# Side products of the attention stages: one clump at the end of each quad's period, in place of four points within it

## The reference, cut to what matters

```
L0: h = layernorm(x)*(1+scale)+shift; q = h Wq; c = h Wkd; k, v = c Wku, c Wvu; rope(q, k)
    y = softmax(mask(q k^T / sqrt(32))) v, 16 heads of 32, causal by blocks of 128; x += y Wo
L1: h = rms(x)*w*(1+scale); q, k, v = h Wq, h Wk, h Wv; rope; 8 heads of 64 on one k and v; x += y Wo
    x += (silu(h Wg) * (h Wu)) Wd
L2: h = layernorm(x)*..+..; q, k, v = h Wqkv; q, k normalised per head; 16 heads of 32
    x += gamma1 * (softmax(q k^T + bias) v Wproj + b);  x += gamma2 * MLP(layernorm(x)..)
L3: per expert: gelu(x W1 + b1) W2 + b2; silu(layernorm(..)) out_W; x += ..
```

## Time and profile before

| | us |
|---|---|
| median of 3 runs | 3025.26 (3024.14 to 3026.44) |
| the profiled execution | 3025.34 |
| its span | 3023.6 |

### The profile page before, as it was taken

One profiled execution on the slowest core, in us unless ns is written; L12 is line 12 of the kernel. 1 busy time (PEld: TensorE's weight loads), 2 busy tenths in 40 slices (PEclk: granted clock), 3 DMA queues, 4 the chain that ended last, 5 costly groups with the idle time before them and its releaser, 6 DMA issues.

```text
span 3023.6 us, 33071 instructions
## 1 busy us (share of the span) xinstructions
PE 2668.8 (88%) x13120; PEld 1592.8 (53%) x13120; DVE 1250.7 (41%) x2490; ACT 1152.7 (38%) x2423; POOL 241.4 (8%) x220
## 2 busy tenths in 40 slices
PE   6588988999999679999996799999997599998787
PEld 1144444544555268888883344444453288885333
DVE  1146545434434444344431346354554544442222
ACT  0256565544434321111112357465664422222332
POOL 2123213101210000000001000000000000001000
PEclk8879999999999889999998799989999799999989
DMA  8000000000000010000001000000000000000000
GB/s 292 14 1 1 1 1 22 1 8 8 8 1 1 21 42 21 22 21 22 22 1 75 1 1 1 1 1 1 1 1 29 14 29 29 15 1 28 14 14 28
DMA packets 33514, 61.27 MB, mean 20 GB/s; under 512 B 3136, under 2 KB 15984, under 8 KB 32848
## 3 DMA queue, kind: packets, MB, share of 16 engines
q1 hardware_dynamic: 29280, 45.63, 4.5%
q0 software_dynamic: 4080, 13.53, 1.2%
HBM read 52.86 MB, written 4.19 MB: 19 GB/s over the span
## 4 chain that ended last, share of the span: by engine, by line
PE 53%; DVE 5%; ACT 4%; issue 1%; POOL 0%; SPq 0%; DMA 0%; DVEq 0%; ACTq 0%; POOLq 0%
PE banks L883 17%; PE banks L896 12%; PE banks L437 8%; PE banks L176 6%; PE banks L611 3%; PE banks L604 2%; DVE sb_Pr L671 2%; PE banks L626 2%; PE banks L81 1%; PE banks L524 1%; PE banks L87 1%; DVE sb_PT L678 1%; DVE sb_Pb L99 1%; ACT sb_hN L124 1%; ACT sb_Pr L696 1%
## 5 line engine op out<-in xcount | busy, mean ns | idle before, releaser
L883 PE MATMUL banks<-sb_H,sb_Ws 128*128 128x512 f32 x2304 | 536.9, 391 | 31.1 <-DVE sb_Ws L934 30.9
L883 PEld LDWEIGHTS banks<-sb_H,sb_Ws 128*128 128x128 f32 x2304 | 435.3, 189 | 123.8 <-issue 32.5
L671 DVE CUSTOM_DVE_ANT_0 sb_Pr<-banks,sb_bias 128x512 f32<-128x512 f32 (+3 forms) x512 | 297.9, 584 | 334.7 <-PE banks L611 334.3
L696 ACT ACTIVATE sb_Pr<-sb_Pr,sb_nmax 128x512 f32<-128x512 f32 (+3 forms) x512 | 327.2, 640 | 153.2 <-DVE sb_nmax L671 147.5
L611 PEld LDWEIGHTS banks<-sb_ident,sb_Pr 128*128 128x128 f32 x2176 | 250.2, 146 | 211.5 <-issue 84.2
L611 PE MATMUL banks<-sb_ident,sb_Pr 128*128 128x128 f32 x2176 | 327.7, 291 | 29.4 <-ACT sb_PT L701 22.3
L604 PE MATMUL banks<-sb_R 32*128 32x512 f32 (+4 forms) x1280 | 313.4, 604 | 33.3 <-DVE sb_nmax L671 17.5
L896 PE MATMUL banks<-sb_hidH,sb_Ws 128*128 128x512 f32 x1024 | 325.3, 389 | 0.0
L701 ACT ACTIVATE sb_PT<-banks 128x512 f32<-128x512 f32 (+3 forms) x320 | 169.0, 528 | 337.1 <-PE banks L611 337.0
L437 PE MATMUL banks<-sb_hN,sb_W 128*128 128x512 f32 x576 | 274.8, 622 | 21.1 <-ACT sb_hN L381 10.6
L678 DVE COPY sb_PT<-banks 128x512 f32<-128x512 f32 (+3 forms) x320 | 194.3, 607 | 123.6 <-PE banks L611 120.6
(11 more groups left out here) (175 smaller groups left out, 2632.0 us busy)
## 6 DMA issues: line engine op xcount, KB each, us to landing
sb_WM<-in_L_cond_Wfc SPq DMA_DIRECT2D x16, 512.0 KB, 4.2
sb_WM<-in_L_cond_Wada SPq DMA_DIRECT2D x6, 1024.0 KB, 5.0
sb_x<-in_x SPq DMA_DIRECT2D x4, 1024.0 KB, 13.7
sb_WM<-in_L_cond_Wg SPq DMA_DIRECT2D x8, 512.0 KB, 3.4
sb_WM<-in_L_cond_Wu SPq DMA_DIRECT2D x8, 512.0 KB, 4.4
sb_WM<-in_L_cond_Wd SPq DMA_DIRECT2D x8, 512.0 KB, 3.6
out_x<-sb_x SPq DMA_DIRECT2D x4, 1024.0 KB, 4.5
sb_W<-in_L_cond_Wqkv POOLq DMA_DIRECT2D x1, 3072.0 KB, 10.6
```

Of the source, the lines that this page charges most:

```text
L671: ins = e.tensor_tensor_reduce(k.Pr[:, n % 4, 0:s.width(u)], S, k.bias[:, s.units[u][2], 0:s.width(u)], -1.0, 3.0e38, ALU.add, ALU.min, s. ...
L696: ins = e.activation(prob, prob if s.biased else k.bank(n % 4)[:, 0:s.width(u)], ACT.Exp, bias=s.stat(k, k.nmax, b, u), scale=-1.0 if s.bi ...
L883: mm = e.matmul(k.bank(s.ups * t + w), lhsT, rhs, start=i == 0, stop=i == len(mats) - 1)
```

## The change

The loop of `weave` keeps one of its four `point(m)` calls, the last one, and a main gets one point for each quad. All operations stay, with their engines, buffers and waits. What changes is the place of each beat in the common list.

```
-        points = 4 * count
+        points = count
         for i, ops in enumerate(sides[1 + m]):
             at_point.setdefault((m, (2 * i + 1) * points // (2 * len(sides[1 + m]))), []).extend(ops)
...
         soft(t + 1, 1)
-        point(m)
         for h, b, c in spreads:
...
                     spreads.append((h, b, g // 2))
-        point(m)
         turn(t, 2)
         turn(t, 3)
         copy(t, 2)
         soft(t + 1, 2)
         copy(t, 3)
         soft(t + 1, 3)
-        point(m)
         point(m)
```

## The result

The changed kernel takes 3129.06 us (median of 4 runs, 3128.91 to 3129.6) against 3025.28: ratio 1.0343, interval 1.0325 to 1.0361, so 104 us slower. The forecast was 3106, 81 slower, with 3055 to 3145 as the range. The direction and the range held. One term was nearly absent: the clumps of short `spread` products in layer 2 were put at 1.6 us, and cost 21 alone and 34 beside the other clumps. Two others were too small with opposite signs, and partly cancelled: the bare turns (step 2) and the covered heads (step 4).

The account below looks back on a forecast made before the run. PE was taken to bound the kernel, busy 88% of the span, so time moves by its idle time, side-by-side scores and the clock. 42 + 23 + 20 - 29 + 13 + 12 = 81 on 3025.34 gave 3106 us, range 3055 to 3145.

Parts of the forecast that it names:

- step 2: Turns 2 and 3 wait uncovered for copies once products leave the early points: +23 us, bounds 10 and 30.
- step 4: 26 quads with nothing or a short product ahead of their scores get a clump there: -29 us, bounds -15 and -45.
- Step 1: 52 new places with two long products in a row, each waiting 0.8 for bank 7's eviction: +42 us, bounds 21 to 52.
- step 5: Norm beats in one clump hold ACT and delay copy 0, so PE stands: +13 us, bounds 0 and 35.
- step 6: Squares of the q and k norm directly ahead of their sum, log and inverse holding copy 0: +12 us, bounds 4 and 20.
- Step 3: Short products in a clump wait for evictions behind DVE's or ACT's softmax work: +20 us, bounds 5 and 35.
- A: Rival: covered heads are worth more, pairs, turns and short products cost less; 3064 us, chance 0.17.
- D: Rival: the softmax chain, not PE, is the path between quads, so only the covered heads count; 2996 us, chance 0.04.
- E: Rival: nothing moves, because consumers take the beats in another order than the list; 3025 us, chance 0.02.
- B: Rival: 10 norms and 3 qk stages cost 2.5 more each, PE coming out at 1.2 GHz; 3139 us, chance 0.12.
- C: Rival: the clock falls in the clumps, a product at 1.2 GHz behind each wait, 52 more; 3158 us, chance 0.07.
- The sign set for a wrong forecast: Product waits below 0.4, or a stretch of projections with a granted clock under 0.9, would show the forecast wrong.

Follow-up runs that it names:

- e1: The changed kernel, but with the q and k norm's spread beats of layer 2 back at their four-point places; 3094.85 us, ratio 1.0231.
- e2: The kernel before, with only the spread beats of layer 2's q and k norm moved into clumps at the end of their period; 3045.92 us, ratio 1.0074.
- e3: The changed kernel, but with the norm beats and the q/k squares, sums, log and inverse at their four-point places, spreads still in clumps; 3110.53 us, ratio 1.0278.
- e4: The changed kernel, but with all projections and output projections back at their four-point places; 3073.93 us, ratio 1.0158.
- e11: The kernel before, with each spread product of q and k written three times into the same bank; 3098.08 us, ratio 1.025.

## Why the prediction was right in direction and 23 us short

**Step 1, long pairs: right in kind, 8 too large.** +42 forecast for 52 pairs; the marked waits for an eviction of a projection or post grew by 34.2 us, and there are 39 more of them. The price of 0.8 was good (54.1 us in 68 waits; 0.69 behind ACT, 0.78 behind DVE in main 9), the number of pairs that show a wait was not. The sign set for it, some 60 waits, came: 62 behind L1212, L1213, L1220 and L1333.

**Step 2, bare turns: too small.** +23 forecast; turns and values wait 49.6 more, of which the norms of step 5 have some 13 (two waits of 7.33 for two of about 1) and step 6 a few more. Where products fill the period it was right: steps 1 and 2 make 7.1 in quads 4 to 9 of main 9, which grew from 76.6 to 84.1, 7.5. What it missed are the quads of short products and norms.

**Step 3, short pairs: this step failed,** at one entry: "0.15 for 11 of qk's spreads (half of one hides beside scores)". It has 1.6 for them. e1 measures 34 and e2, the same clumps by themselves, 21. The rest of the step was right: the waits of and for rope products grew by some 20 (L470 from 2.7 to 17.4, L437 for L478 from 3.4 to 8.8), where 18.4 was forecast. The working counted what the second product waits for and took the rest of the quad as unchanged. In the trace after, more than half of the loss (19.9 of 35.7) is busy time of the same instructions at a clock of 0.67 to 0.73, where before had 1.00, 0.81 and 1.00; the other 15.8 is idle time, itself ten times the 1.6. The paragraph on the clock named the danger for the qk stage, but put it in the range with 10 and not in the sum. Its reason, the 1.00 beside a 0.69 wait in the earlier trace rows, speaks for clumps of projections and was right there; it says nothing on quads whose products take 1.0 and are followed by waits as long as themselves. How much of the loss is the fall of the clock and how much follows from the waits without it stays open: e2 moves both together. e3 adds that the same clumps cost 15 less when the norms and the q/k sums ahead of them are spread out.

**Step 4, covered heads: right in kind, half in size.** -29 forecast. The waits of L604 alone gave 24.1 and the scores' busy time 36.3, some of the latter by layer 1's higher clock. The working took 26 quads as bare and all others as fully covered. The earlier trace rows are the ends of a range, 2.77 and 1.14, and many quads lay between: layer 0's scores were busy 86.8 and now 68.1. No wait marks such a quad; the mean busy time of the group per quad does.

**Step 5, norm: right in kind in layer 2, wrong in sign in layer 1.** The wait of 7 to 8 us came as drawn. PE in after, main 9:

```profile
1925.04 1.93 PE L626 MATMUL banks<-sb_PT,sb_V 128*32 128x256 f32 x32
1934.30 1.94 PE L611 MATMUL banks<-sb_ident,sb_Pr 128*128 128x128 f32 x8 [7.33 <-ACT sb_PT L701]
1936.04 4.92 PE L437 MATMUL banks<-sb_hN,sb_W 128*128 128x512 f32 x8
```

and what ACT does in that time:

```profile
1923.78 1.28 ACT L375 ACT_TABLE_LOAD   x1
...
1927.07 0.63 ACT L378 ACTIVATE sb_Pb<-sb_Pb 128x512 f32<-128x512 f32 x1
1928.52 2.71 ACT L381 ACTIVATE sb_hN<-sb_hN,sb_mod 128x512 f32<-128x512 f32 x4 [0.82 <-DVE sb_hN L402]
1931.14 2.54 ACT L385 ACTIVATE sb_x<-sb_x,sb_comb 128x512 f32<-128x512 f32 x4
1933.58 0.57 ACT L701 ACTIVATE sb_PT<-banks 128x512 f32<-128x512 f32 x1
```

The turns wait for copy 0 (L701), which is ready at once but stands behind inverse, shift and `extra` in ACT's order. Quads 1 to 3 of main 9 grew from 31.98 to 39.96 and those of main 10 by 8.5, against the 5 forecast for each; their clock fell from 0.95 to 0.87. For mains 4 to 6 of layer 1 the forecast was +7.5; e3 shows their norms in a clump 12 better than at four points, since the wait for the exp goes. Layer 1 as a whole rose by 5, with 15.2 for its 19 pairs (0.8 each), 2 for its turns and 7.5 for its norms in the forecast before heads are taken off. Its scores alone gave back 25 (12.6 busy, 12.2 waits), close to the -29 for all three layers.

**Step 6, norm of q and k: right for the waits.** Three waits of 4.8 forecast, 2.5 more each; L518 waits 15.8 us in four, the longest 4.6, where it waited 8.3. The quads of the sums grew by 3.0, 3.9 and 5.4 in mains 8, 9 and 10, 12.3 against 7.5; the other 4.4 of the step lie in the quad behind them.

**The balance.** What e1, e3 and e4 undo cannot be added up, since 15 of e3's lie in the quads of e1. By quads, from the start times of the scores, nothing is counted twice. Of the 104, the twelve spread quads have 36 (forecast about 6: the 1.6 and the 4.4 of step 6), the norm quads of mains 9 and 10 have 16.5 (forecast 10), the quads of the sums 12.3 (forecast 7.5). All else has 39, where some 57 was left of the forecast: the heads, which gave back more than was priced, are among it. The errors are +30, +6.5, +5 and -18, together the 23 by which the forecast was short. So part of its nearness is luck: a term that was nearly absent stands against one that was too small the other way.

**The rivals.** A (3064) had the direction of both its terms: the pairs gave 34, nearer to its 30 than to 42, and the heads more than its 40. Its total is 65 short, since it took the turns and the short products still lower. D (2996) and E fall with the 55 of e4. B (3139) is nearest in number. By its mechanism each norm and q/k stage costs 2.5 more with PE at a lower clock: the norms of mains 9 and 10 do (3.0 and 3.5 more than forecast, at 0.87), the three q/k stages in part (1.6 each), and in layer 1 norms in clumps are 12 cheaper than at four points. C (3158) is wrong at its place, the projections; its kind of event, a clock that falls in clumps, took place in the twelve spread quads. The sign set for a wrong forecast did not show: the product quads 4 to 9 of main 9 in after ran at 1.00.

## What to carry to other kernels

A clump costs the turnaround of its one bank per pair, here 0.7 to 0.8 us, and that can be counted from a single pair in the trace. Before counting, look at the clumps whose products are as short as the wait between them: there the waits are no longer small against the work, and in layer 2 PE's clock fell with them. Count what a cover is worth from the busy time of side-by-side matmuls, not from marked waits alone. The best spacing follows what waits in each stage (the exp, the turns, the head), so choose it per stage and test each alone: here that gave 3011 us, 0.3% under the kernel before.

## What the runs showed of the hardware that was not expected

- Waits of 0.69 to 0.78 between products of 3.6 left the granted clock at 1.00 (1990 to 2020 us of after). Spread products of 1.0 with waits of 0.8 to 1.3 between them, in quads that also wait for turns, ran at 0.67 to 0.75 in after and in e2, and at 0.75 to 0.82 in e3, where only the beats ahead differ.
- The clock moved up as well, in layer 1 from 0.97 to 1.00 with the clumps.
- Full work behind a fall did not bring the clock back at once: in e11 it stayed at 1.2 GHz for 23.9 us (2029.15 to 2053.05) with PE busy all of the time.
- The same order of work can meet a fall of the clock or not: 35.53 us at 0.81 in main 9 and 30.46 at 1.00 in main 10 of before, and in e1 31.86 at 0.95 and 36.71 at 0.81, the other way round.
- Four scores that find their data one after another take 2.75 in place of 1.14 and show it as busy time, not as a wait.
